# Self attention in a four-layer decoder: scores of four heads from split queries and keys in two float32r passes

## The chip, the cores and the metric

The kernel runs on one core of a Trainium2 chip, as one program. TensorE (PE in the rows, PEld for its weight loads) multiplies, VectorE (DVE) and ScalarE (ACT) read its results from eight PSUM banks, GpSimd (POOL) does small work, and SyncE (SP) issues transfers. The metric is the device time of one execution in microseconds; lower is better.

## The reference, cut to what matters

The reference is a decoder of four layers, each a cross attention and an FFN with experts. Only one piece is touched: the self attention that opens the second layer's FFN block. For each of 16 batches of 112 tokens with 256 channels (16 heads of 16):

```
h = layernorm(x, ln1_g, ln1_b)
qkv = (h @ Wqkv).reshape(Bb, Tt, H, 3 * hd)
q, k = (rope(q), rope(k))      # concat([t1*cos - t2*sin, t1*sin + t2*cos])
scores = jnp.einsum('bqhd,bkhd->bhqk', q, k) / math.sqrt(hd)
scores = jnp.where(causal, scores, -1e9)
probs = jax.nn.softmax(scores, axis=-1)
attn = jnp.einsum('bhqk,bkhd->bqhd', probs, v).reshape(Bb, Tt, d) @ Wproj
x = x + attn
```

## The kernel before

The stage `self_attention` lies at 950 to 1194 us of the profiled execution. It handles the 16 batches one after another; the heads of a batch go in four groups (g) of four. Each engine has an order written out by hand: `first` fills the pipeline, `heads(b, ...)` is run once a batch, and within it work on four batches is interleaved: scores, softmax and values of batch b, scores of groups 0 and 1 of b+1, normalisation and projection of b+2, first statistics of b+3, output of b-1. Counters (semaphores) join the engines; each engine takes its instructions strictly in its written order.

What happens to a batch, with the lines that count here:

- `project_qk` (PE, L2754) writes queries and keys of all heads to one bank; DVE's `rotate` (L2988 to L2992) applies the rotary embedding into `turned_q`.
- `turn_rotated` (PE, L2773) transposes `turned_q` in four pieces of 128 channels, two of queries and two of keys, so that channels lie on the rows. `take_queries` (ACT, L2897) copies the queries' half to `qT`.
- `spread_keys` (DVE, L3001) builds `keys`: for each of 16 heads a copy of the eight-head block of keys, multiplied by `headmask`, which is 0.25 on the head's own 16 rows and 0 on the others. With that a plain product over all 128 rows gives one head's scores, and the moving side carries four heads side by side (448 columns).
- `scores(b, g)` (PE) adds the causal mask by a bfloat16 product with the identity (L2786) and then the float32 product of `qT` and `keys` (L2788); the trace shows that one as two instructions.
- `group_max` (DVE, L3009) takes the maximum per head, `exps` (ACT, L2911) the exponential, `turn` and `take_probsT` (PE L2795, ACT L2918) transpose the probabilities, `values` (PE, L2807) multiplies with the values. `divide` (L3016, L3018), `turn_outputs`, `take_outputs`, `output` and `add` (L3027, L3029) finish the batch; `norm_1` to `norm_3` (L1038 to L1042, L2966), `turn_tokens` (PE, L2745) and `take_tokens` (ACT, L2886) prepare the next ones.

Two places in the written order matter. On DVE, `heads(b)` has `group_max(b, 2)`, `spread_keys(b+1)`, `group_max(b, 3)` in a row, and later `group_max(b+1, 0)`, `rotate(b+2)`, `group_max(b+1, 1)`, `norm_2(b+3)`, `add(b-1)`, `divide(b)`, `norm_3(b+3)`. On ACT the order is `exps(b, 2)`, `take_queries(b+1)`, `take_probsT(b, 1)`, `take_outputs(b-1)`, `exps(b, 3)`, `take_tokens(b+2)`; `project_qk(b+2)` waits for the last of these.

Of the kernel before, what the change touches and what calls it, by code (L numbers as in the profile page):

```python
# [6 lines left out]
F32 = mybir.dt.float32  # L7
# [3 lines left out]
F32R = mybir.dt.float32r  # L11
# [7 lines left out]
P = 128  # L19
# [2652 lines left out]
def self_attention(nc, core, name):  # L2672
# [8 lines left out]
    with ctx:  # L2681
# [8 lines left out]
        qT = [sb(f"qT{i}", [P, DC, T]) for i in range(2)]  # L2690
        keys = [sb(f"keys{i}", [P, H, T]) for i in range(2)]
# [18 lines left out]
        keys_ready, q_ready = core.counter("taken_K"), core.counter("taken_Q")  # L2710
        made = {c: core.counter(f"made_{c}") for c in "LVOY"}
# [11 lines left out]
        with nc.Block() as block:  # L2723
# [10 lines left out]
            def _(pe):  # L2734
# [13 lines left out]
                def project_qk(b):  # L2748
# [3 lines left out]
                    pe.wait_ge(rope_done.sem, rope_done.at(b.n))  # L2752
                    for k in range(DC):
                        ins = pe.matmul(psQK[0:T, 0:2 * D], hT[:, k, :], wqkv[:, k, 0:2 * D],  # L2754
                                        start=(k == 0), stop=(k == DC - 1))
# [10 lines left out]
                def turn_rotated(b, before_):  # L2766
# [5 lines left out]
                    for c in range(2 * DC):  # L2772
                        ins = pe.transpose(psR[:, c * T:(c + 1) * T],  # L2773
                                           turned_q[:, c * 8:(c + 1) * 8, :].rearrange("t h e -> t (h e)"),
                                           core.ident[0:T, 0:T])
                    ins.then_inc(r_made.sem, 1)

                def scores(b, g):
                    if g == 0:

                        pe.wait_ge(q_ready.sem, q_ready.at(b.n + 1))
                        pe.wait_ge(keys_ready.sem, keys_ready.at(b.n + 1))
# [5 lines left out]
                    pe.matmul(psS[g % 2][0:T, 0:G * T], qT[b.par][:, g // 2, :], keys[b.par][:, G * g:G * g + G, :],  # L2788
# [88 lines left out]
            def _(act):  # L2877
# [17 lines left out]
                def take_queries(b):  # L2895
                    act.wait_ge(r_made.sem, r_made.at(b.n + 1))
                    act.activation(qT[b.par][:, :, :], psR[:, 0:DC * T].rearrange("p (c t) -> p c t", t=T), ACT.Copy)\  # L2897
                        .then_inc(q_ready.sem, 1)
# [56 lines left out]
            def _(dve):  # L2955
# [24 lines left out]
                def rotate(b):  # L2980
# [4 lines left out]
                    def all_heads(t, lo, hi):  # L2985
# [6 lines left out]
                    dve.tensor_tensor(turned_q[:, :, :], turned_q[:, :, :], turned_by[:, :, :], ALU.add)\  # L2992
                        .then_inc(rope_done.sem, 1)

                def spread_keys(b):

                    dve.wait_ge(r_made.sem, r_made.at(b.n + 1))

                    dve.wait_ge(q_ready.sem, q_ready.at(b.n + 1))
                    for c in range(DC):  # L3000
                        ins = dve.tensor_tensor(keys[b.par][:, 8 * c:8 * c + 8, :],  # L3001
# [340 lines left out]
```

## Time and profile before

| | us |
|---|---|
| median of 3 runs | 3431.1 (3428.69 to 3436.66) |
| the profiled execution | 3437.43 |
| its span, first to last instruction | 3435.6 |
| self attention within it | about 950 to 1194 |
| PE, DVE, ACT busy over the whole span | 3106.0, 1658.8, 1563.6 |
| mean granted TensorE clock (1 is full) | 0.948 |

The stage is 7% of the time, and nothing outside of it changes but the numbers in a small table. So the whole-program shares say little about it; what has to be read is one period of the stage, from one `project_qk` to the next, engine by engine.

### The profile page before, as it was taken

What the parts mean: (1) busy time and instruction counts of PE and PEld (TensorE: products, weight loads), DVE (VectorE), ACT (ScalarE), POOL (GpSimd) and SP (SyncE); (2) the same over time, 40 slices, a digit from 0 to 9 for tenths busy, and PEclk for the clock granted to TensorE, in tenths of its full rate; (3) what the DMA queues carried; (4) which work ended last, traced back from release to release, by engine and by line L of the source; (5) the groups of instructions that cost most, each with busy time, mean ns of one, the idle gap of its engine ahead of it and who ended that gap; (6) DMA issues with size and microseconds to landing.
All of it is one profiled execution on the core that took longest, in us unless ns stands there. A gap on an engine that the chain in (4) does not pass through costs nothing. (4 is left out here: it accounts for less than half of the span.)

```text
span 3435.6 us, 60328 instructions
## 1 busy us (share of the span) xinstructions
PE 3106.0 (90%) x21966; PEld 2609.6 (76%) x21966; DVE 1658.8 (48%) x3470; ACT 1563.6 (46%) x4177; POOL 1319.2 (38%) x1417
## 2 busy tenths in 40 slices
PE   5888858998989869899999999598999999997999
PEld 4776748996756559778888887488788888876998
DVE  4777760003566557544444444301444444445766
ACT  2554523443345435445555555244555555552232
POOL 0000001112100022167777777211577777773433
PEclk8999969999999869999999999699999999996999
DMA  5555535552100044200000000464000000001332
GB/s 143 135 132 128 131 134 198 183 183 74 50 1 1 4 165 141 66 20 15 12 14 14 15 13 1 168 217 138 13 13 12 12 13 13 12 1 53 114 106 89
DMA packets 146134, 253.21 MB, mean 74 GB/s; under 512 B 46892, under 2 KB 122664, under 8 KB 133304
## 3 DMA queue, kind: packets, MB, share of 16 engines
q1 hardware_dynamic: 132216, 223.67, 21.7%
q0 software_dynamic: 8064, 20.20, 2.1%
q10 hardware_dynamic: 5568, 5.51, 0.5%
q8 instruction: 183, 3.00, 0.4%
q14 instruction: 103, 0.84, 0.1%
HBM read 214.85 MB, written 34.46 MB: 73 GB/s over the span
## 5 line engine op out<-in xcount | busy, mean ns | idle before, releaser
L719 POOL TENSOR_SCALAR L_probs<-L_probs,L_inverse 112x375 f32<-112x375 f32 x512 | 653.0, 1275 | 119.3 <-issue 119.3
L867 DVE TENSOR_REDUCE L_negmax<-bank 112x1 f32<-112x375 f32 x768 | 394.7, 542 | 428.1 <-PE bank L471 356.3
L675 ACT ACTIVATE L_probs<-bank,L_negmax 112x375 f32<-112x375 f32 x768 | 435.2, 572 | 216.7 <-DVE L_negmax L867 211.9
L498 PE MATMUL bank<-ident,L_probs 112*125 112x112 f32 x2304 | 399.4, 282 | 19.2 <-POOL L_probs L719 12.9
L498 PEld LDWEIGHTS bank<-ident,L_probs 112*125 112x125 f32 x2304 | 338.0, 189 | 91.1 <-issue 49.6
L717 POOL TENSOR_TENSOR L_inverse<-L_sums,neg_one 112x1 f32<-112x1 f32 x512 | 297.2, 580 | 141.4 <-ACT L_probs L675 141.1
L655 ACT ACTIVATE L_probsT<-bank 125x336 f32<-125x336 f32 x512 | 231.9, 453 | 248.4 <-PE bank L498 248.3
L637 ACT ACTIVATE v<-bank 125x512 f32<-125x512 f32 x192 | 114.8, 598 | 266.6 <-PE bank L424 266.6
L705 POOL TENSOR_TENSOR L_stats<-L_stats,neg_half 112x1 f32<-112x1 f32 x48 | 27.0, 563 | 520.6 <-DVE L_stats L784 520.6
L513 PE MATMUL bank<-L_probsT,v 125*64 125x112 f32 x3072 | 206.7, 270 | 1.8 <-ACT L_probsT L655 1.1
L417 PE MATMUL bank<-L_ctx_hi,L_wk_hi 128*128 128x376 f32 x512 | 149.5, 373 | 30.2 <-DVE L_ctx_lo L851 22.7
L513 PEld LDWEIGHTS bank<-L_probsT,v 125*64 125x64 f32 x3072 | 152.0, 138 | 31.0 <-issue 1.7
L1613 ACT ACTIVATE L0t_hidden<-bank,L0t_b 128x128 f32<-128x128 f32 x280 | 102.3, 368 | 143.6 <-PE bank L1578 126.0
L675 ACT ACTIVATION_READ_ACCUMULATOR L_probs<-bank,L_negmax 112x1 f32 x768 | 152.8, 199 | 0.0
L1578 PEld LDWEIGHTS bank<-L0t_xT,L0t_w 128*128 128x128 f32 x1120 | 133.3, 195 | 10.5 <-issue 8.8
L1578 PE MATMUL bank<-L0t_xT,L0t_w 128*128 128x128 f32 x1120 | 133.8, 279 | 8.0 <-issue 8.0
L809 DVE SCALAR_TENSOR_TENSOR L_keys_lo<-bank,L_bk,L_keys_hi 128x376 fp32r<-128x376 f32 x128 | 76.4, 607 | 131.8 <-ACT L_keys_hi L627 131.8
L1629 DVE TENSOR_TENSOR L0t_ys<-bank,L0t_b 128x256 f32<-128x256 f32 x35 | 14.9, 425 | 258.3 <-PE bank L1590 258.3
L424 PE MATMUL bank<-L_wv_hi,L_ctx_hi 128*125 128x512 f32 x384 | 137.8, 440 | 0.0
L809 DVE SCALAR_TENSOR_TENSOR L_keys_lo<-bank,L_keys_hi 128x376 fp32r<-128x376 f32 x128 | 68.8, 547 | 132.4 <-ACT L_keys_hi L627 131.9
L417 PE MATMUL bank<-L_ctx_hi,L_wk_lo 128*128 128x376 f32 x512 | 131.8, 339 | 0.0
L417 PE MATMUL bank<-L_ctx_lo,L_wk_hi 128*128 128x376 f32 x512 | 131.3, 338 | 0.0
(327 smaller groups left out, 7109.2 us busy)
## 6 DMA issues: line engine op xcount, KB each, us to landing
L0t_w<-in_F_w SPq DMA_DIRECT2D x35, 1024.0 KB, 4.9
L_keys<-spread_k SPq DMA_DIRECT2D x64, 376.0 KB, 6.7
L2t_w<-in_F_w SPq DMA_DIRECT2D x21, 1024.0 KB, 4.9
L_ctxT<-in_ctxT SPq DMA_DIRECT2D x48, 375.0 KB, 3.1
w_all<-in_F_w SPq DMA_DIRECT2D x16, 1024.0 KB
cap_w<-in_F_w SPq DMA_DIRECT2D x16, 1024.0 KB, 5.2
L3d_row<-comb_rows SPq DMA_DIRECT2D x64, 224.0 KB, 3.2
L_q<-spread_q SPq DMA_DIRECT2D x128, 56.0 KB, 2.2
```

The costliest lines, as they stand in the source:

```text
L417: ins = pe.matmul(bank[:, 0:SP], wt[:, k, m * P:(m + 1) * P], c[b.par][:, k, :], start=(n + k == 0), stop=(n + k == DC + 1))
L424: ins = pe.matmul(bank[0:SJ, 0:VW], c[b.par][:, k, j * SJ:(j + 1) * SJ], wt[:, k, vn * VW:(vn + 1) * VW], start=(n + k == 0), stop=(n + k ...
L498: ins = pe.transpose(psT[h % len(psT)][0:SJ, j * T:(j + 1) * T], probs[h % NB][:, j * SJ:(j + 1) * SJ], core.ident[0:T, 0:T])
L513: ins = pe.matmul(bank[i * dh:(i + 1) * dh, at:at + T], v[b.par][0:SJ, j, (h + i) * dh:(h + i + 1) * dh], probsT[(h + i) % NT][:, j, :], s ...
L637: ins = act.activation(v[b.par][0:SJ, j, n * VW:(n + 1) * VW], bank[0:SJ, 0:VW], ACT.Copy)
L655: act.activation(probsT[h % NT][:, :, :], psT[h % len(psT)][0:SJ, 0:J * T].rearrange("p (j t) -> p j t", t=T), ACT.Copy)\
L675: act.activation(probs[e % NB][:, :], psS[e % 2][0:T, 0:S], ACT.Exp, bias=negmax[b.par][:, e:e + 1], accum_out=sums[b.par][:, e:e + 1]).th ...
L717: pool.tensor_tensor(inverse[b.par][:, h:h + 1], sums[b.par][:, h:h + 1], core.neg_one[0:T, :], ALU.pow)
L719: pool.tensor_scalar(probs[h % NB][:, :], probs[h % NB][:, :], inverse[b.par][:, h:h + 1], None, ALU.mult)\
L809: dve.scalar_tensor_tensor(out=keys_lo[b.par][:, m, :], in0=bank[:, 0:SP], scalar=bk[:, m:m + 1] if biased else 0.0, in1=keys_hi[b.par][:, ...
L867: dve.tensor_reduce(negmax[b.par][:, h:h + 1], psS[h % 2][0:T, 0:S], AX, ALU.max, negate=True).then_inc(maxed.sem, 1)
L1578: ins = pe.matmul(psH[f % 4][:, 0:tile], w1[t % 2][:, k, f * P:(f + 1) * P], xT[:, k, :], start=(k == 0), stop=(k == DC - 1))
```

## The change

The float32 product of the scores becomes two products of float32r operands. The queries are split into a rounded part `q_hi` and the rest `q_lo`. A group's four heads are 64 channels; the rounded keys go to rows 0 to 63 and the rest of the keys to rows 64 to 127 of one operand. `q_hi` holds the same 64 channels on both halves of the rows, so that one pass gives q_hi times both parts of the keys, and a second pass over 64 rows adds q_lo times the rounded keys. For this the last instruction of `rotate` writes each group's channels twice (`twice`, 1024 elements a row in place of 512), `turn_rotated` has eight transposes in place of four (queries into the bank of `project_qk`, keys into the old one), ACT makes two rounded copies of 448 columns where it made one copy of 224, and DVE subtracts twice (64 rows) and multiplies by `headmask` in four pieces of 448 from SBUF in place of two of 896 from PSUM. The number of elements of `keys` is the same. `scores` waits for the keys group by group, and `project_qk` of the next batch also waits for `q_lo`, since the bank is shared.

```diff
@@ project_qk
                     pe.wait_ge(rope_done.sem, rope_done.at(b.n))
+                    pe.wait_ge(q_ready.sem, q_ready.at(b.n))
@@ turn_rotated
-                    for c in range(2 * DC):
-                        ins = pe.transpose(psR[:, c * T:(c + 1) * T],
-                                           turned_q[:, c * 8:(c + 1) * 8, :].rearrange("t h e -> t (h e)"),
-                                           core.ident[0:T, 0:T])
-                    ins.then_inc(r_made.sem, 1)
+                    for at, bank in ((0, psQK), (HG, psR)):
+                        for g in range(HG):
+                            ins = pe.transpose(bank[:, g * T:(g + 1) * T],
+                                               twice[:, at + g, :, :].rearrange("t i e -> t (i e)"), core.ident[0:T, 0:T])
+                        ins.then_inc(r_made.sem, 1)
@@ scores
                         pe.wait_ge(q_ready.sem, q_ready.at(b.n + 1))
-                        pe.wait_ge(keys_ready.sem, keys_ready.at(b.n + 1))
+                    pe.wait_ge(keys_ready.sem, keys_ready.at(HG * b.n + g + 1))
...
-                    pe.matmul(psS[g % 2][0:T, 0:G * T], qT[b.par][:, g // 2, :], keys[b.par][:, G * g:G * g + G, :],
+                    pe.matmul(psS[g % 2][0:T, 0:G * T], q_hi[b.par][:, g, :], keys[b.par][:, G * g:G * g + G, :],
+                              start=False, stop=False)
+                    pe.matmul(psS[g % 2][0:T, 0:G * T], q_lo[b.par][:, g, :], keys[b.par][0:64, G * g:G * g + G, :],
                               start=False, stop=True).then_inc(scored.sem, 1)
@@ take_queries
-                    act.wait_ge(r_made.sem, r_made.at(b.n + 1))
-                    act.activation(qT[b.par][:, :, :], psR[:, 0:DC * T].rearrange("p (c t) -> p c t", t=T), ACT.Copy)\
-                        .then_inc(q_ready.sem, 1)
+                    act.wait_ge(r_made.sem, r_made.at(2 * b.n + 1))
+                    act.activation(q_hi[b.par][:, :, :], psQK[:, 0:HG * T].rearrange("p (g t) -> p g t", t=T), ACT.Copy)\
+                        .then_inc(q_high.sem, 1)
+                    act.wait_ge(r_made.sem, r_made.at(2 * b.n + 2))
+                    act.wait_ge(keys_ready.sem, keys_ready.at(HG * b.n))
+                    act.activation(k_pair[:, :, :], psR[:, 0:HG * T].rearrange("p (g t) -> p g t", t=T), ACT.Copy)\
+                        .then_inc(k_high.sem, 1)
@@ rotate
-                    dve.tensor_tensor(turned_q[:, :, :], turned_q[:, :, :], turned_by[:, :, :], ALU.add)\
-                        .then_inc(rope_done.sem, 1)
+                    straight, crossed = (t[:, :, :].rearrange("t (g h) e -> t g (h e)", h=G).unsqueeze(2)
+                                         .broadcast_to([T, 2 * HG, 2, 64]) for t in (turned_q, turned_by))
+                    dve.tensor_tensor(twice[:, :, :, :], straight, crossed, ALU.add).then_inc(rope_done.sem, 1)
@@ spread_keys
-                    dve.wait_ge(r_made.sem, r_made.at(b.n + 1))
-                    dve.wait_ge(q_ready.sem, q_ready.at(b.n + 1))
-                    for c in range(DC):
-                        ins = dve.tensor_tensor(keys[b.par][:, 8 * c:8 * c + 8, :],
-                                                psR[:, (DC + c) * T:(DC + c + 1) * T].unsqueeze(1).broadcast_to([P, 8, T]),
-                                                headmask[:, :].unsqueeze(2).broadcast_to([P, 8, T]), ALU.mult)
-                    ins.then_inc(keys_ready.sem, 1)
+                    dve.wait_ge(q_high.sem, q_high.at(b.n + 1))
+                    dve.tensor_tensor(q_lo[b.par][:, :, :], psQK[0:64, 0:HG * T].rearrange("p (g t) -> p g t", t=T),
+                                      q_hi[b.par][0:64, :, :].bitcast(F32), ALU.subtract).then_inc(q_ready.sem, 1)
+                    dve.wait_ge(k_high.sem, k_high.at(b.n + 1))
+                    low = k_pair[64:P, :, :]
+                    dve.tensor_tensor(low, psR[64:P, 0:HG * T].rearrange("p (g t) -> p g t", t=T), low.bitcast(F32),
+                                      ALU.subtract)
+                    dve.drain()
+                    for g in range(HG):
+                        dve.tensor_tensor(keys[b.par][:, G * g:G * g + G, :],
+                                          k_pair[:, g, :].bitcast(F32).unsqueeze(1).broadcast_to([P, G, T]),
+                                          headmask[:, 0:G].unsqueeze(2).broadcast_to([P, G, T]), ALU.mult)\
+                            .then_inc(keys_ready.sem, 1)
```

On DVE, in the part of `heads` from the maximum of group 2 to that of group 1 of the next batch, the program of before has these rows (negmax rows are `group_max`, the `turned` rows `rotate`, the `stats` rows `norm_1`):

```order
L3009 TENSOR_REDUCE L1s_negmax0<-bank4 112x4
L3001 TENSOR_TENSOR L1s_keys1<-bank3,self_headmask_12 128x896 x2
L3009 TENSOR_REDUCE L1s_negmax0<-bank5 112x4
L1038 BN_STATS L1s_stats<-x 112x6
L1040 BN_AGGR L1s_stats<-L1s_stats 112x2
L1042 TENSOR_SCALAR L1s_stats<-L1s_stats 112x1
L3009 TENSOR_REDUCE L1s_negmax1<-bank4 112x4
L2988 TENSOR_TENSOR L1s_turned_by<-bank1,self_sin_10 112x32x8
L2989 TENSOR_TENSOR L1s_turned_by<-bank1,self_sin_10 112x32x8
L2990 TENSOR_TENSOR L1s_turned_q<-bank1,self_cos_9 112x512
L2992 TENSOR_TENSOR L1s_turned_q<-L1s_turned_q,L1s_turned_by 112x512
L3009 TENSOR_REDUCE L1s_negmax1<-bank5 112x4
```

The changed program has, in the same place:

```order
L3029 TENSOR_REDUCE L1s_negmax0<-bank4 112x4
L3012 TENSOR_TENSOR L1s_q_lo1<-bank1,L1s_q_hi1 64x448
L3017 TENSOR_TENSOR L1s_k_pair<-bank3,L1s_k_pair 64x448
L3021 TENSOR_TENSOR L1s_keys1<-L1s_k_pair,self_headmask_12 128x448 x4
L3029 TENSOR_REDUCE L1s_negmax0<-bank5 112x4
L1038 BN_STATS L1s_stats<-x 112x6
L1040 BN_AGGR L1s_stats<-L1s_stats 112x2
L1042 TENSOR_SCALAR L1s_stats<-L1s_stats 112x1
L3029 TENSOR_REDUCE L1s_negmax1<-bank4 112x4
L3001 TENSOR_TENSOR L1s_turned_by<-bank1,self_sin_10 112x32x8
L3002 TENSOR_TENSOR L1s_turned_by<-bank1,self_sin_10 112x32x8
L3003 TENSOR_TENSOR L1s_turned_q<-bank1,self_cos_9 112x512
```

Nothing has changed its place; two instructions between the maxima of groups 2 and 3 have become six. The row that follows these is the doubled last step of `rotate`, `L1s_twice`, 112x1024.

On ACT, from the exponentials of group 2 to the copy of the normalised tokens, before:

```order
L2911 ACTIVATE L1s_probs0<-bank4,L1s_negmax0 112x112 x4
L2897 ACTIVATE L1s_qT1<-bank3 128x224
L2918 ACTIVATE L1s_probsT1<-bank6 112x448
L2903 ACTIVATE L1s_oT<-bank0 128x224
L2911 ACTIVATE L1s_probs1<-bank5,L1s_negmax0 112x112 x4
L2886 ACTIVATE L1s_hT<-bank0,self_b_8,self_g_7 128x112 x2
```

and in the changed program:

```order
L2924 ACTIVATE L1s_probs0<-bank4,L1s_negmax0 112x112 x4
L2905 ACTIVATE L1s_q_hi1<-bank1 128x448
L2910 ACTIVATE L1s_k_pair<-bank3 128x448
L2931 ACTIVATE L1s_probsT1<-bank6 112x448
L2916 ACTIVATE L1s_oT<-bank0 128x224
L2924 ACTIVATE L1s_probs1<-bank5,L1s_negmax0 112x112 x4
L2894 ACTIVATE L1s_hT<-bank0,self_b_8,self_g_7 128x112 x2
```

One copy of 224 columns has become two of 448 ahead of the copy of the transposed probabilities.

## Rows read from the trace of the kernel before

**Rows 1.** Windows: one period; busy us (instructions) of each engine, then PE clock, DMA
```profile
1041.90:1056.19 14.29, 13.11 (x80) 9.34 (x80) 9.78 (x23) 7.88 (x26) 1.08 (x2) 1.00 0.00 1
```

**Rows 2.** Timeline, PE, one period: start us, duration us, engine, line, operation
```profile
1044.53 1.97 PE L2754 MATMUL bank<-self_wqkv,L1s_hT 128*112 128x512 f32 x4
...
1054.30 0.92 PE L2788 MATMUL bank<-L1s_keys,L1s_qT 128*112 128x448 f32 x2
1055.05 0.55 PE L2795 MATMUL bank<-ident,L1s_probs 112*112 112x112 f32 x4
1056.52 0.38 PE L2745 MATMUL bank<-ident,L1s_normed 112*128 112x112 f32 x2 [0.93 <-issue]
...
1058.82 0.68 PE L2754 MATMUL bank<-self_wqkv,L1s_hT 128*112 128x512 f32 x1
```

**Rows 3.** Timeline, DVE, the same period
```profile
1046.54 0.42 DVE L2988 TENSOR_TENSOR L1s_turned_by<-bank,self_sin 112x256 f32<-112x256 f32 x1 [1.57 <-PE bank L2754]
...
1047.21 0.68 DVE L2990 TENSOR_TENSOR L1s_turned_q<-bank,self_cos 112x512 f32<-112x512 f32 x1
1047.97 0.69 DVE L2992 TENSOR_TENSOR L1s_turned_q<-L1s_turned_q,L1s_turned_by 112x512 f32<-112x512 f32 x1
1048.58 0.62 DVE L3009 TENSOR_REDUCE L1s_negmax<-bank 112x4 f32<-112x448 f32 x1
...
1052.25 0.62 DVE L3009 TENSOR_REDUCE L1s_negmax<-bank 112x4 f32<-112x448 f32 x1
1054.35 2.09 DVE L3001 TENSOR_TENSOR L1s_keys<-bank,self_headmask 128x896 f32<-128x896 f32 x2 [1.48 <-ACT L1s_qT L2897]
1056.36 0.61 DVE L3009 TENSOR_REDUCE L1s_negmax<-bank 112x4 f32<-112x448 f32 x1
```

**Rows 4.** Timeline, ACT, the same period
```profile
1052.92 1.08 ACT L2911 ACTIVATE L1s_probs<-bank,L1s_negmax 112x112 f32<-112x112 f32 x4
1053.87 0.38 ACT L2897 ACTIVATE L1s_qT<-bank 128x224 f32<-128x224 f32 x1
1055.63 0.55 ACT L2918 ACTIVATE L1s_probsT<-bank 112x448 f32<-112x448 f32 x1 [1.38 <-PE bank L2795]
1056.07 0.35 ACT L2903 ACTIVATE L1s_oT<-bank 128x224 f32<-128x224 f32 x1
1057.01 1.09 ACT L2911 ACTIVATE L1s_probs<-bank,L1s_negmax 112x112 f32<-112x112 f32 x4 [0.58 <-DVE L1s_negmax L3009]
1057.97 0.80 ACT L2886 ACTIVATE L1s_hT<-bank,self_b,self_g 128x112 f32<-128x112 f32 x2
```

**Rows 5.** Lines L860 and L856: duration ns min/median/max, first and last start
```profile
L860 DVE TENSOR_TENSOR L_q_low<-L_q,L_q_high x64: 624/625/881, 1468.5 to 3069.9; 128x448 fp32r<-128x448 f32 x64
L856 DVE CAST L_q_high<-L_q x64: 393/394/727, 1468.0 to 3066.2; 128x448 fp32r<-128x448 f32 x64
```

**Rows 6.** Timeline, PE, expert stage: float32r passes of 448 columns
```profile
3251.52 0.37 PE L2275 MATMUL bank<-L3d_hid_hi,dense_w_hi 128*128 128x448 f32 x1
3251.73 0.37 PE L2275 MATMUL bank<-L3d_hid_lo,dense_w_hi 128*128 128x448 f32 x1
```

**Rows 7.** Timeline, PE: the first work after three idle stretches elsewhere
```profile
304.16 0.37 PE L484 MATMUL bank<-L_barred,ident_b 112*112 112x376 bf16 x1 [2.53 <-DMA L_q<-spread_q]
...
2426.66 0.61 PE L417 MATMUL bank<-L_ctx_hi,L_wk_hi 128*128 128x376 f32 x2 [1.88 <-DVE L_keys_lo L809]
...
1499.89 0.58 PE L498 MATMUL bank<-ident,L_probs 112*125 112x112 f32 x3 [1.74 <-POOL L_probs L719]
```

**Rows 8.** Windows around and behind these (columns as in rows 1)
```profile
304.10:307.60 3.50, 3.44 (x9) 2.25 (x10) 1.73 (x5) 0.67 (x2) 0.78 (x2) 0.56 0.12 45
...
2424.00:2428.00 4.00, 2.12 (x11) 1.45 (x9) 2.88 (x8) 2.15 (x6) 1.32 (x3) 0.95 0.00 0
2428.00:2432.00 4.00, 4.00 (x20) 3.45 (x20) 1.92 (x4) 2.40 (x7) 3.64 (x5) 0.62 0.02 4
...
1500.00:1504.00 4.00, 4.00 (x32) 2.94 (x33) 0.48 (x2) 1.05 (x2) 3.66 (x5) 1.00 0.00 0
```

More of the change, by code:

```diff
@@ L2689, in self_attention @@
         turned_by, turned_q = sb("turned_by", [T, 2 * H, 16]), sb("turned_q", [T, 2 * H, 16])
-        qT = [sb(f"qT{i}", [P, DC, T]) for i in range(2)]
-        keys = [sb(f"keys{i}", [P, H, T]) for i in range(2)]
+        q_hi = [sb(f"q_hi{i}", [P, HG, T], F32R) for i in range(2)]
+        q_lo = [sb(f"q_lo{i}", [P // 2, HG, T], F32R) for i in range(2)]
+        k_pair = sb("k_pair", [P, HG, T], F32R)
+        keys = [sb(f"keys{i}", [P, H, T], F32R) for i in range(2)]
+        twice = sb("twice", [T, 2 * HG, 2, 64])
         causal_b = sb("causal_b", [T, T], BF16)
@@ L2710, in self_attention @@
         keys_ready, q_ready = core.counter("taken_K"), core.counter("taken_Q")
+        q_high, k_high = core.counter("q_split"), core.counter("k_high")
         made = {c: core.counter(f"made_{c}") for c in "LVOY"}
@@ L3078, in self_attention @@
             s.stage_over(2 * B)
-        for s in (normed_ready, o_ready, qk_made, rope_done, r_made, keys_ready, q_ready, *made.values(), *taken.values()):
+        for s in (normed_ready, o_ready, qk_made, rope_done, q_high, k_high, q_ready, *made.values(), *taken.values()):
             s.stage_over(B)
+        r_made.stage_over(2 * B)
+        keys_ready.stage_over(HG * B)
         for s in (scored, maxed, exped, turned, probsT_ready, pv_done):
@@ L3265, in lay_out @@
     a["keys"] = np.arange(S, dtype=np.float32)
-    a["headmask"] = np.where(np.arange(P)[:, None] // 16 == np.arange(8)[None, :], 0.25, 0.0).astype(np.float32)
+    a["headmask"] = np.where(np.arange(P)[:, None] % 64 // 16 == np.arange(8)[None, :], 0.25, 0.0).astype(np.float32)
     for n in ("wq", "wk", "wv", "wo"):
```

## The prediction

> **What bounds the kernel now.** First the windows of one period of the stage: 14.29 us, of which TensorE is busy 13.11, 92%, and VectorE 9.78, 68% [rows 1]. Taken by busy time TensorE is the bound, and the change takes work from it. I did not stop there, because TensorE still stands idle 1.18 us in every period, always at the same places (0.93 us of it before `turn_tokens` [rows 2]); an engine that bounds a loop does not. The Trainium skill (Perfetto Trace Analysis, Identifying the Most-Contended Engine) says that matmul busy time is no good measure and to take the weight loads' share instead; here that is 9.34 us, 65%, which would put VectorE first. That is the same suspicion, but shares don't settle it either way.
>
> So next the timelines of the three engines over one period, followed link by link from `project_qk` to the next `project_qk`, each step from start to start:
>
> 1. `project_qk` starts on PE at 1044.53, `rotate` on DVE at 1046.54: 2.01.
> 2. `rotate`, 1046.54 to the start of `group_max(b+1, 1)` at 1048.58: 2.04.
> 3. From there DVE works without a gap up to the start of `group_max(b, 2)` at 1052.25, and the exponentials of that group start on ACT at 1052.92: 4.34. (It ends at 1052.87.)
> 4. The exponentials, 1052.92 to 1053.87, when the queries' copy starts behind them: 0.95.
> 5. The copy, to the start of `spread_keys` on DVE at 1054.35: 0.48.
> 6. `spread_keys`, to 1056.36: 2.01.
> 7. `group_max(b, 3)`, queued behind it on DVE; exponentials of group 3 at 1057.01; `take_tokens` at 1057.97; the next `project_qk` at 1058.82: 2.46.
>
> The sum is 14.29, the whole period [rows 2 to 4]. This loop closes through DVE and ACT; of PE it has only `project_qk`. The score passes, the transposes of probabilities and the value products aren't in it: they wait at `project_qk`, or at `turn_tokens`, for the loop. Both idle stretches of DVE (1.57 us waiting for `project_qk`, 1.48 us waiting for the queries' copy [rows 3]) are waits of the loop itself.
>
> **The change part by part.**
>
> *Scores (off the loop).* A float32 product of 448 columns takes 0.75 us (1054.30 to 1055.05 [rows 2]); a float32r pass of 448 columns takes 0.21 (3251.52 to 3251.73 [rows 6]). Two passes in place of it: 0.75 - 0.42 = 0.33 saved, four groups, 1.3 us a batch. The second pass has 64 rows; no row prices it apart, so I bound it by one wide pass and by the old 0.37 of half a float32 product. Either end changes nothing, since no score is on the loop.
>
> *Transposes (off the loop).* Four of the same kind (L2795) last 0.55, less what overlaps the next instruction [rows 2]. Four more cost 0.4 to 0.55 a batch; I take 0.4. PE's work goes from 13.1 to about 12.2 us a batch.
>
> *Last step of `rotate` (on the loop, link 2).* DVE's two-operand instruction takes 0.61 from start to start at 512 elements (1047.97 to 1048.58) and 2.01/2 = 1.005 at 896 [rows 3]: 1.03 ns an element. 512 more elements cost 0.53.
>
> *The queries' copy (link 5).* ACT copies 448 columns in 0.55, 224 in 0.38 [rows 4]: 0.17 more before DVE may start. The keys' copy follows at 0.44 (1055.63 to 1056.07); it ends 0.44 + 0.55 = 0.99 after the first one starts, and DVE needs it at 0.65 + 0.54 = 1.19. Hidden.
>
> *`spread_keys` (link 6).* At 448 elements an instruction takes 0.61 - 64 x 1.03 ns = 0.54 from start to start (the split's subtraction of another stage lasts 0.625 in all [rows 5], the same thing with the end that overlaps the next). Now: `q_lo` 0.54; `low` with the drain behind it 0.62 + 0.08 = 0.70 (the drain's 0.08 as between 1047.89 and 1047.97 [rows 3]); four products 4 x 0.54 = 2.16. In all 3.40 for 2.01: 1.39 more. That 64 rows in place of 128 save nothing I assume: every row works side by side, and there is no row with fewer; if it halved them it would be 0.5 less. The Trainium skill (VectorE: DVE Perf Modes, Two Vector instructions with no wait between them) has it that an instruction whose operands start in another quarter of the rows waits until all earlier ones are finished; `low` starts at row 64. No row here shows such a pair; by that rule the overlap of 0.08 is lost once more a batch, about 1 us in all.
>
> *New waits.* `project_qk(b+2)` waits for `q_lo(b+1)`, done 5 us earlier. `scores(b+1, 0)` waits for its own quarter of the keys; it comes behind `values(b, 1)`, late enough. The keys' copy waits for the last batch's keys, long done. The real queue is on DVE: `group_max(b, 3)` stands behind all six instructions, though its scores have been ready for a microsecond, and behind it wait `exps(b, 3)`, `take_tokens` and `project_qk`.
>
> *Sum of a lap.* 0.53 + 0.17 + 1.39 = 2.09; the period becomes 16.38 us. The loop is run for each `project_qk` in `heads`, 14 times: +29.3 us. Filling and draining the pipeline have one `spread_keys` more and cheaper scores; I take these as even, within 2 us.
>
> *The clock (added by the longer wait).* How long PE now idles before `project_qk`: counted from the start of the first copy, the probabilities' copy starts at 0.88 (two copies of 0.44); from its start to `turn_tokens` it was 0.89 (1055.63 to 1056.52) and from there to `project_qk` 2.30, now 1.97 with the cheaper score [rows 2, 4]. PE is free at 3.74. The loop arrives at 0.65 + 3.40 + 2.46 = 6.51. PE idles 2.8 us each lap, where it had nothing. What such gaps did in this trace: behind 2.53 and 1.88 us the granted clock fell to the lower level (1.2 of 2.4 GHz), 0.56 over the next 3.5 us in one case, 0.95 then 0.62 in the other; behind 1.74 us it stayed at 1.00 [rows 7, 8]. So I expect it to fall in most laps. The first case lost (1 - 0.56) x 3.5 = 1.5 us of PE's work at once; in the second, 0.05 x 4 = 0.2 us was lost before 2428, so it fell some 0.4 us before that, 0.9 after the restart. The first 1.8 us behind the gap are `project_qk`, which is on the loop: 1.5 us lost in the first manner, 0.9 in the second, nothing where the clock holds. What is slow behind it (`values`, a score) has over a microsecond to spare until `group_max(b+1, 1)`. I take 1.0 a lap, bounds 0 and 1.8: +14 us, bounds 0 and 25.
>
> *Total.* 29.3 + 14 = 43.3. Against the profiled execution, 3437.4, that is 3480.7. The median of the runs shown is 6.3 us lower, 3431.1, so for the median: 3474.4.
>
> **The rivals.**
>
> *A, the loop with a full clock:* +29.3, 3460.4. For it: the two low stretches came in other stages, and the work around the gap here is dense float32. Against: a gap of 1.88 was enough, and this one is 2.8.
>
> *B, the products into float32r run at the pace of a cast:* a cast of 448 elements lasts 0.394 where the subtraction lasts 0.625 [rows 5]. If the four products did so, 4 x 0.23 = 0.92 a lap is saved, the lap grows by 1.17, the total is +16.4 at full clock, 3447.5. Against it: the subtraction in that row also writes float32r, and is at the slow pace. The Trainium skill (VectorE: DVE Perf Modes, The perf-mode tier table) gives float32 two-operand instructions one element a cycle from SBUF as from PSUM, and the double pace only to those of one operand; by that B does not happen.
>
> *C, TensorE was the bound after all, and it gets faster:* then a lap falls by PE's saving, 1.3 - 0.4 = 0.9, 15 us over 16 batches, 3416. Place: PE's order between `project_qk` and the next. It decides only if the loop of DVE and ACT is shorter than PE's work, so from 13.1 us on down; I have it at 14.29 and growing. For it speaks the 92%; against it, that the seven links add up to the period without a rest.
>
> *D, no change:* some of the added DVE work would have to fall into DVE's own idle time (3.9 us a lap) without delaying `group_max(b, 3)`. The order rules it out: all of it stands before that instruction. Should a float32r pass cost 0.37, as half a float32 product, that still gives PE 13.5 us of work in a lap of 16.4: no change to my number.
>
> **How the numbers follow.** My forecast (loop and clock) 0.62; A 0.22; B 0.06; C 0.05; the rest 0.05, most of it between B and no change. The low end, 3455, holds A with a few microseconds less; the high end, 3488, is 29.3 + 25 with 2 or 3 us for the skill's rule and the ends of the stage. Outside are B, C and D and a longer tail above. 0.2% of the time is 7 us, about what can be told from no change here. Slower by more: forecast, A, B and most of the rest less some doubt, 0.91; no change 0.04; faster 0.05.
>
> **What the profile after would show.** Right: a period of some 17 us in the stage (16.4 where the clock holds); PE idle 2.5 to 3 us before `project_qk`, released by ACT's `hT`; `group_max(b, 3)` starting some 3.4 us after `q_lo`; the `twice` instruction at 1.2 us, the products at 0.6; float32r passes 0.21 apart; windows of 0.5 to 0.6 in PE's clock behind that gap. Wrong: a period under 14.3, PE idle time gone, or the gap before `project_qk` under a microsecond; then link 7 did not carry the delay. If the period grows but the clock stays at 1.00, only the last term was wrong.

## The result and the profile after

The changed kernel takes 3518.1 us (median of 4 runs, 3511.6 to 3524.7) and the kernel before 3431.1 (4 runs, 3428.7 to 3436.7): a ratio of 1.0258, 95% interval 1.0243 to 1.0272. It is slower, as predicted, but by 87 us and not by 43, and outside the predicted range (3455 to 3488). The profiled execution took 3515.3 with a span of 3513.5, 77.9 more than the profiled one before (which was 6 us above its median, where this one is 3 below); the granted clock over the whole span fell from 0.948 to 0.925.

The windows say where that is. The first row is one lap, from one `project_qk` to the next, and answers to [rows 1]; then come the steady laps, the filling and the draining of the pipeline.

```profile
1095.16:1115.20 20.04, 17.48 (x84) 11.72 (x84) 11.98 (x26) 8.27 (x27) 1.09 (x2) 0.76 0.00 1
1000.00:1230.00 230.00, 205.74 (x996) 138.40 (x995) 139.84 (x305) 98.56 (x306) 12.49 (x23) 0.76 0.00 1
950.00:1000.00 50.00, 42.02 (x155) 26.52 (x153) 28.89 (x60) 17.35 (x54) 2.71 (x5) 0.64 0.00 1
1230.00:1278.00 48.00, 41.04 (x192) 29.39 (x192) 18.54 (x37) 17.42 (x55) 0.00 (x0) 0.68 0.00 1
```

The same view of the kernel before, for its two ends (the second from its last `turn_tokens` to the next stage; between the ends the clock is 1.00):

```profile
950.00:1000.00 50.00, 41.89 (x217) 27.30 (x218) 33.19 (x72) 22.21 (x72) 3.80 (x7) 0.94 0.00 1
...
1157.22:1196.05 38.83, 32.83 (x188) 24.17 (x188) 14.66 (x29) 16.79 (x54) 0.00 (x0) 0.86 0.00 1
```

The lap was 14.29 and is now about 20 us, and the clock column has gone from 1.00 to 0.76. By the starts of `turn_tokens` the stage divides as follows. From its first one to the first of the steady laps it took 948.63 to 985.07 before and 946.75 to 996.66 after: 13.5 us more. Twelve laps took 172.1 (to 1157.22) and take 233.6 (to 1230.25): 61.4 more, 19.47 us a lap on average, in single laps 17.2 to 20.7. From there to the first instruction of the next stage, 38.8 and 48.0: 9.2 more. That is 84 us in this stage. It began 1.9 earlier, and the rest of the program gave back 4.

TensorE over one such lap:

```profile
1095.16 3.75 PE L2759 MATMUL bank<-self_wqkv,L1s_hT 128*112 128x512 f32 x4 [2.22 <-ACT L1s_hT L2894]
...
1105.62 0.35 PE L2792 MATMUL bank<-L1s_causal_b,ident_b 112*112 112x448 bf16 x1
1105.64 0.52 PE L2794 MATMUL bank<-L1s_keys,L1s_q_hi 128*112 128x448 f32 x1
1106.10 0.46 PE L2796 MATMUL bank<-L1s_keys,L1s_q_lo 64*112 64x448 f32 x1
1106.49 0.60 PE L2803 MATMUL bank<-ident,L1s_probs 112*112 112x112 f32 x4
...
1111.14 0.38 PE L2749 MATMUL bank<-ident,L1s_normed 112*128 112x112 f32 x2 [0.93 <-issue]
...
1115.20 2.05 PE L2759 MATMUL bank<-self_wqkv,L1s_hT 128*112 128x512 f32 x2 [1.63 <-ACT L1s_hT L2894]
```

The new wait before `project_qk` is there, released by ACT's `hT`. Behind it `project_qk` takes 3.75 us instead of the 1.97 of [rows 2]. The granted clock around it in short windows:

```profile
1092.80:1093.60 0.80, 0.14 (x2) 0.00 (x0) 0.80 (x2) 0.25 (x1) 0.00 (x0) 0.97 0.00 0
1093.60:1094.40 0.80, 0.00 (x0) 0.00 (x0) 0.65 (x4) 0.80 (x5) 0.18 (x1) 0.50 0.00 0
...
1103.40:1104.00 0.60, 0.60 (x5) 0.44 (x3) 0.31 (x2) 0.60 (x4) 0.00 (x0) 0.68 0.00 0
1104.00:1113.00 9.00, 8.07 (x59) 6.05 (x57) 6.17 (x14) 3.76 (x11) 0.55 (x1) 1.00 0.00 1
```

It falls to the lower level, 1.2 GHz, already inside the gap, and comes back at about 1103.8: ten microseconds low, half the lap, with TensorE busy all the time from 1095.16 on. A mean of 0.76 over the steady laps says the same of all of them: 48% of the time at half clock, 9.3 us of each 19.47. (Not all laps look alike: in some, as at about 1032.1, 1073.1 and 1151.6, the clock falls already around `turn_tokens`, and the gap before `project_qk` is then at most 0.5 us.) What this does on DVE and ACT:

```profile
1098.95 0.42 DVE L3001 TENSOR_TENSOR L1s_turned_by<-bank,self_sin 112x256 f32<-112x256 f32 x1 [4.29 <-PE bank L2759]
...
1101.74 0.62 DVE L3029 TENSOR_REDUCE L1s_negmax<-bank 112x4 f32<-112x448 f32 x1
...
1106.60 0.62 DVE L3029 TENSOR_REDUCE L1s_negmax<-bank 112x4 f32<-112x448 f32 x1 [0.50 <-PE bank L2796]
1109.12 0.62 DVE L3012 TENSOR_TENSOR L1s_q_lo<-bank,L1s_q_hi 64x448 fp32r<-64x448 f32 x1 [1.90 <-ACT L1s_q_hi L2905]
...
1112.73 0.62 DVE L3029 TENSOR_REDUCE L1s_negmax<-bank 112x4 f32<-112x448 f32 x1
```

```profile
1102.67 0.54 ACT L2931 ACTIVATE L1s_probsT<-bank 112x448 f32<-112x448 f32 x1 [6.14 <-PE bank L2803]
...
1107.57 1.08 ACT L2924 ACTIVATE L1s_probs<-bank,L1s_negmax 112x112 f32<-112x112 f32 x4
1108.52 0.57 ACT L2905 ACTIVATE L1s_q_hi<-bank 128x448 fp32r<-128x448 f32 x1
```

The seven links of this lap are 3.79, 2.79, 5.83, 0.95, 0.60, 3.61 and 2.47; the sum is 20.04. Links 4, 5 and 7 are as forecast (0.95, 0.65, 2.46), link 6 is 0.2 longer than its 3.40. Link 1 is `project_qk` at half clock. Link 2 is 0.22 over its 2.57. Link 3, which I had as DVE alone (4.34), now waits for TensorE: `exps(b, 1)` stands on ACT behind the copy of transposes that TensorE made late, and `group_max(b, 2)` itself waits 0.50 for a score pass.

### The profile page after: what moved, and what is told of

Same layout as the page of the kernel before. It is cut to its first block and busy times, and to the rows that moved or that the text cites. A ratio compares the mean times of both kernels' runs of the same rounds, so it can differ in the third digit from the quotient of the medians.

```text
span 3513.5 us, 60600 instructions
## 1 busy us (share of the span) xinstructions
PE 3172.1 (90%) x22030; PEld 2650.8 (75%) x22030; DVE 1703.5 (48%) x3534; ACT 1570.3 (45%) x4193; POOL 1315.9 (37%) x1417
## 6 DMA issues: line engine op xcount, KB each, us to landing
w_all<-in_F_w SPq DMA_DIRECT2D x16, 1024.0 KB, 13.5
```

## The experiments

The question is where the 3 us a lap beyond the forecast loop come from: the loop is longer than its links said, or the clock costs three times what I took. Then, what lets the clock fall. The four sessions ran the kernel before again, at 3429.7 (runs 1 to 4), 3434.3 (5 to 8), 3431.5 (9 to 11) and 3429.7 (12); each ratio is against its own session. Line numbers differ by a few between kernels.

**1. The gap before `project_qk` filled** with twelve bf16 products into its own bank.

```diff
 def project_qk(b):
-    pe.wait_ge(taken["L"].sem, taken["L"].at(b.n + 1))
     pe.wait_ge(rope_done ...)
     pe.wait_ge(q_ready ...)
+    for _ in range(12):
+        pe.matmul(psQK[0:T, 0:G * T], ident_b, causal_b x 4, start=True, stop=True)
+    pe.wait_ge(taken["L"].sem, taken["L"].at(b.n + 1))
```

> The changed kernel with 12 extra bfloat16 products of 448 columns (0.19 us each, 2.2 us) into the bank of project_qk, issued while TensorE would idle before project_qk; their results are overwritten. Theory 'clock': the gap lets the granted clock fall, the low stretch lasts about 10 us of every 20 us lap and carries everything beyond the lengthened loop; filled, the clock stays at 1.00, the lap is the 16.4 us of the links and the time is before + 29, about 3460. Rival 'other waits' (the extra 2.7 us a lap are waits of DVE and ACT that only look like clock): the time stays at about 3518, or grows with the extra work.

Measured: 3511.6, ratio 1.0238 (1.0219 to 1.0256), some 7 us less than the changed kernel and hardly to be told from it (the two intervals overlap). The theory missed by 50 us, and the rival's number is near without its reason. The gap is closed, and the clock falls all the same:

```profile
1070.97 0.38 PE L2749 MATMUL bank<-ident,L1s_normed 112*128 112x112 f32 x2 [0.93 <-issue]
...
1073.59 3.72 PE L2757 MATMUL bank<-L1s_causal_b,ident_b 112*112 112x448 bf16 x12
```

```profile
1072.00:1073.00 1.00, 1.00 (x5) 0.48 (x5) 1.00 (x3) 0.00 (x0) 0.00 (x0) 0.89 0.06 16
1073.00:1076.00 3.00, 3.00 (x11) 2.06 (x11) 1.94 (x6) 2.19 (x8) 0.54 (x1) 0.50 0.00 0
1076.00:1078.00 2.00, 2.00 (x9) 1.11 (x8) 0.00 (x0) 0.99 (x5) 0.00 (x0) 0.95 0.00 0
```

It goes at about 1072.8, 1.8 us after the end of the 0.93 us before `turn_tokens` that had been there all along. In this lap it is low for some 3.4 us, in the next (from about 1089.9) for 6.8; laps alternate between 18.0 and 19.6. So one filled gap is not enough, and my picture of one gap with one stretch behind it is wrong.

**2. In the changed kernel, `group_max(b, 3)` ahead of `spread_keys(b + 1)`.** This takes the added DVE work out of the way of the last maximum.

```diff
 group_max(b, 2)
+group_max(b, 3)
 if after:
     spread_keys(b + 1)
-group_max(b, 3)
```

> The changed kernel with group_max(b, 3) ahead of spread_keys(b+1) on DVE, nothing else. Theory 'loop': project_qk hangs on group_max(b, 3), which no longer waits behind the six instructions; its links shrink by 0.54 + 0.70 + 2.16 = 3.4 us, TensorE's own work and its wait at turn_tokens set the lap, about 13.5 to 14, so the time is 5 to 10 us under before: 3421 to 3426, if the clock holds. If the gap at turn_tokens (some 1.5 us) is enough to drop the clock, up to 40 more. Rival 'DVE is simply too full' (its total work bounds the lap, whatever the order): stays within 10 us of 3518.

Measured: 3472.7, ratio 1.0132 (1.0107 to 1.0158): 45 us back, which rules out the rival, and still 7 us above what the theory allowed with a clock that falls. Idle time before `project_qk` is gone, and some laps are 14.4 us (1064.54 to 1078.95); others are up to 17.6, where the clock falls. One such place:

```profile
1076.36 0.38 PE L2749 MATMUL bank<-ident,L1s_normed 112*128 112x112 f32 x2 [0.93 <-issue]
...
1078.95 3.49 PE L2759 MATMUL bank<-self_wqkv,L1s_hT 128*112 128x512 f32 x4
```

Its only idle stretches are 0.93 and 0.10 us, hardly more than the kernel before has, where the clock held.

**3. The same step in the kernel before.**

> The kernel before with group_max(b, 3) ahead of spread_keys(b+1). Theory 'loop': the old order had the keys ready just as TensorE wanted them (scores of b+1 start 1.1 us after the keys end), so delaying the keys behind the maximum, which must wait for its scores until 1055.3, moves them 1.5 us later and TensorE waits about 0.4 us a lap: 3437, slightly slower. Rival 'this order is better anyway': faster by the 0.05 us a lap or more that project_qk waits, 3420 to 3430.

Measured: 3452.3, ratio 1.0065 (1.0046 to 1.0083), 15 us above the theory's 3437: the 0.4 us a lap came as expected, the fall of the clock was not expected. From `turn_tokens` to `turn_tokens` a lap is 14.70 where the clock holds (1042.76 to 1057.45 is one) and 16.38 where it falls (1057.45 to 1073.83), five and seven of twelve; the clock over 1000 to 1150 is 0.93. It falls behind a second short wait of 0.35 us that stands beside the 0.93.

**4. The kernel before, its two key products issued twice** with a drain between: 2.16 us more on the loop and nothing else.

```diff
-for c in range(DC):
+for c in 2 * list(range(DC)):          # a drain ahead of the second round
     ins = dve.tensor_tensor(keys[...], psR[...], headmask[...], ALU.mult)
```

> The kernel before with the two products that build the keys issued twice (the same values, a drain between): DVE's part of the loop grows by 2.1 us a lap, as much as the change adds, while TensorE's work stays that of before (float32 scores). Theory 'loop': +2.1 x 14 = +29 at a full clock, 3460; and TensorE then idles about 2.1 us before project_qk, over the 1.9 us behind which the clock was seen to fall, so with the clock as in the changed kernel up to +90, 3520. Rival 'it is the float32r passes or the new copies': then this kernel stays within 10 us of before.

Measured: 3477.6, ratio 1.0142 (1.0122 to 1.0161), 48 us more. On DVE the products and the drain take 4.17 us from their start to `group_max(b, 3)` (995.38 to 999.55), where they took 2.01:

```profile
995.38 4.25 DVE L3004 TENSOR_TENSOR L1s_keys<-bank,self_headmask 128x896 f32<-128x896 f32 x4 [1.49 <-ACT L1s_qT L2897]
```

Three laps of the profile are 16.45 or 16.46 (985.56 to 1002.01 is one), which is 14.29 + 2.16: the loop passes added DVE work on in full. Other laps are 17 to 21, and the clock over 1000 to 1150 is 0.90. So the same delay without any part of the change does more than half of its damage (48 of 87 us).

**5. The changed kernel with both gaps filled:** the twelve products, and five ahead of `turn_tokens`.

```diff
 if after2:
+    pe.wait_ge(exped.sem, exped.at(HG * b.n + 3))
+    for _ in range(5):
+        pe.matmul(psS[0][0:T, 0:G * T], ident_b, causal_b x 4, start=True, stop=True)
     turn_tokens(b + 2, prior)
```

> The changed kernel with the 12 extra products before project_qk and 5 more (0.9 us) in the idle time before turn_tokens, into a score bank that is free then; all of them are overwritten. Theory 'thin stretch' (formed on the run with one gap filled, in which the clock fell at the scores behind turn_tokens, ahead of the filled gap: the changed kernel does too little TensorE work around turn_tokens, where the float32 score of before did more): with both filled the clock stays at 1.00, the lap is the 16.4 us of the links, time before + 29, 3460. Rival 'the fillers only add work': 3510 or more, as with one gap filled.

Measured: 3486.0, ratio 1.0147 (1.0121 to 1.0173). The first row is a lap, the second the steady stretch, the others the two ends:

```profile
1065.39:1081.95 16.56, 16.56 (x103) 11.45 (x102) 11.70 (x26) 8.50 (x27) 1.08 (x2) 1.00 0.00 1
...
1000.00:1193.00 193.00, 192.72 (x1180) 133.48 (x1179) 136.05 (x303) 98.34 (x301) 12.43 (x23) 1.00 0.00 1
...
950.00:1000.00 50.00, 44.75 (x213) 29.60 (x212) 29.33 (x61) 19.05 (x59) 2.97 (x6) 0.85 0.00 1
1193.00:1240.00 47.00, 42.16 (x204) 30.44 (x203) 18.41 (x36) 17.58 (x56) 0.00 (x0) 0.69 0.00 1
```

The time lies between the theory's 3460 and the rival's 3510: the laps are nearly as the theory had them, the ends of the stage are not. With the clock at 1.00 the lap is 16.56 by measurement and 16.38 by the prediction's links. This run separates the two terms: of the 5.2 us that a lap grew, 2.27 are the loop and 2.9 the clock. (TensorE has no idle time left in this lap, but link 7 is 2.48 where it was 2.47 in the changed kernel, so the products do not hold `project_qk` up.) The links of this lap are read from its DVE and ACT rows:

```profile
1067.40 0.42 DVE L3007 TENSOR_TENSOR L1s_turned_by<-bank,self_sin 112x256 f32<-112x256 f32 x1 [2.50 <-PE bank L2761]
...
1069.97 0.62 DVE L3035 TENSOR_REDUCE L1s_negmax<-bank 112x4 f32<-112x448 f32 x1
...
1075.86 0.62 DVE L3018 TENSOR_TENSOR L1s_q_lo<-bank,L1s_q_hi 64x448 fp32r<-64x448 f32 x1 [1.59 <-ACT L1s_q_hi L2911]
1076.51 0.63 DVE L3023 TENSOR_TENSOR L1s_k_pair<-bank,L1s_k_pair 64x448 fp32r<-64x448 f32 x1
1077.21 2.23 DVE L3027 TENSOR_TENSOR L1s_keys<-L1s_k_pair,self_headmask 128x448 fp32r<-128x448 f32 x4
1079.47 0.62 DVE L3035 TENSOR_REDUCE L1s_negmax<-bank 112x4 f32<-112x448 f32 x1
```

```profile
1074.30 1.09 ACT L2930 ACTIVATE L1s_probs<-bank,L1s_negmax 112x112 f32<-112x112 f32 x4 [0.47 <-DVE L1s_negmax L3035]
1075.27 0.56 ACT L2911 ACTIVATE L1s_q_hi<-bank 128x448 fp32r<-128x448 f32 x1
```

**6. Run 2 with the five products ahead of `turn_tokens`.**

> The changed kernel with group_max(b, 3) ahead of spread_keys(b+1), and the 5 extra products before turn_tokens. Theory 'thin stretch': the clock stays at 1.00 nearly throughout, the lap is 13.5 to 14.3 and the time 3420 to 3431, where the same order without the fillers took 3473. Rival 'DVE and ACT bound this order': 3460 to 3475, the fillers change nothing.

Measured: 3448.9, ratio 1.0040 (1.0024 to 1.0057). The clock is 1.00 over 1000 to 1150 and every lap 14.33. Of the 43 us that run 2 still lost, products that compute nothing give back two thirds. The rest, which the theory did not have, is at the ends of the stage: in the profiles the twelve steady laps take 172.0 us (172.1 in the kernel before), the filling 6.5 more and the draining 9.0 more.

**7. Run 6 with `group_max(b, 2)` also moved ahead of `norm_3(b + 2)`.**

> As the run before, with group_max(b, 2) also ahead of norm_3(b+2). Theory 'loop': 0.3 us a lap less before the exponentials of group 2, 3416 to 3427; the best version that the links point to. Rival: norm_3 later makes TensorE wait at turn_tokens instead, no gain over the run before.

Measured: 3449.3, ratio 1.0041 (1.0027 to 1.0054). No gain over run 6, and laps of 14.33 again: with the maxima out of the way of `spread_keys` the DVE order is not what sets the lap. What does set the 14.33, no run tests.

**8. The kernel before with cheaper scores alone:** `qT` and `keys` held as float32r, each float32 product replaced by two float32r passes of the same operands. The remaining parts of the operands are left out, and DVE and ACT do what they did.

```diff
-pe.matmul(psS[g % 2][...], qT[...], keys[...], start=False, stop=True).then_inc(scored.sem, 1)
+for last in (False, True):
+    ins = pe.matmul(psS[g % 2][...], qT[...], keys[...], start=False, stop=last)
+ins.then_inc(scored.sem, 1)
```

> The kernel before with queries and keys held as float32r and the score product as two float32r passes of the same operands: the remaining parts are left out and the product is added twice, so the scores are another thing. DVE's and ACT's instructions, their number and size stay those of before; only TensorE's work falls, by 0.33 us a group. Theory 'thin stretch': with nothing added anywhere, the cheaper scores alone let the clock fall in many laps, and the time rises by 10 to 50 us. Rival 'only the long gap before project_qk does it': the clock stays at 1.00 and the time within 5 us of before.

Measured: 3444.0, ratio 1.0026 (1.0008 to 1.0044). Cheaper scores make the kernel slower, by some 9 us (0.1 to 0.4%), just under the theory's 10 to 50. Where the clock holds, the laps are 14.28 or 14.29 (985.29 to 999.58 to 1013.86), no shorter than before; what TensorE saves turns into idle time before `project_qk`, and behind it the clock falls in some laps, which are then 15.7:

```profile
999.58 1.97 PE L2754 MATMUL bank<-self_wqkv,L1s_hT 128*112 128x512 f32 x4 [1.12 <-ACT L1s_hT L2888]
...
1005.65 0.35 PE L2786 MATMUL bank<-L1s_causal_b,ident_b 112*112 112x448 bf16 x1
1005.68 0.73 PE L2789 MATMUL bank<-L1s_keys,L1s_qT 128*112 128x448 f32 x2
1006.25 0.55 PE L2797 MATMUL bank<-ident,L1s_probs 112*112 112x112 f32 x4
```

The laps are only part of the loss. The first row is the steady stretch; the second goes from the last `turn_tokens` to the next stage, and the third is the same stretch of run 12, where the freed time is filled:

```profile
1000.00:1150.00 150.00, 129.17 (x803) 99.55 (x802) 97.10 (x220) 79.87 (x254) 10.82 (x20) 0.93 0.00 1
...
1160.21:1205.81 45.60, 38.47 (x188) 30.89 (x188) 15.72 (x31) 16.69 (x54) 0.00 (x0) 0.66 0.00 1
...
1159.85:1195.28 35.43, 29.31 (x204) 23.38 (x204) 14.53 (x30) 16.75 (x54) 0.00 (x0) 0.98 0.00 1
```

Twelve laps take 5.4 us more than before, the drain 6.8 more: it is 45.6 us at a clock of 0.66, where the kernel before has 38.8 at 0.86 and run 12 has 35.4 at 0.98.

**9. The changed kernel with only the five products ahead of `turn_tokens`,** the counterpart of run 1.

> The changed kernel with five short bf16 products ahead of turn_tokens only; the 2.5 us before project_qk stay empty. What each gap does by itself. Theory (the clock falls wherever TensorE's work is thin for long enough; both places matter): the gap before project_qk alone still lets it fall in most laps, behind the gap, in project_qk: laps of 17 to 20 us, window 1000:1190 at 0.80 to 0.95, time 3500 to 3515. Rival (only the thin stretch around turn_tokens starts the fall): laps 16.5 and the clock at 1.00 without the twelve products, time 3480 to 3488, as with both gaps filled.

Measured: 3522.5, ratio 1.0277 (1.0262 to 1.0293), above theory and rival and not to be told from the changed kernel. From the fifth lap on all are 20.4 or 20.5, so that filling this gap alone even lengthens them (19.47 on average in the changed kernel). In 0.5 us windows the clock falls at 1046, after less than a microsecond of idling in the gap before `project_qk`:

```profile
1045.00:1045.50 0.50, 0.10 (x2) 0.00 (x0) 0.40 (x2) 0.50 (x3) 0.00 (x0) 1.00 0.00 0
1045.50:1046.00 0.50, 0.00 (x0) 0.00 (x0) 0.45 (x2) 0.50 (x4) 0.21 (x1) 0.97 0.00 0
1046.00:1046.50 0.50, 0.00 (x0) 0.00 (x0) 0.24 (x1) 0.50 (x3) 0.33 (x1) 0.50 0.00 0
```

With runs 1 and 5: either gap by itself lets the clock fall, and in the changed kernel both have to be closed.

**10. Run 8 with the five products ahead of `turn_tokens`.**

> The kernel before with each float32 score product replaced by two float32r passes of the same operands (the remaining parts are left out, nothing is added on DVE or ACT), and five bf16 products ahead of turn_tokens. Without the five it took 3444, 9 us more than before. Theory (those 9 us are the clock alone): it stays at 1.00 in 1000:1150, laps 13.6 to 14.3, time 3425 to 3436. Rival (the 9 us come from something else in the two passes, as a start later behind them): time unchanged, 3440 to 3447, with the clock at 1.00.

Measured: 3438.7, ratio 1.0019 (1.0008 to 1.0030), clock 0.97 over 1000 to 1150. It still falls in some laps (1055.60 to 1071.31 is one, 15.71 us), where the 1.1 us before `project_qk` is still open; the others are about 14.28. The time lies between the theory and the rival, and both had the clock at 1.00. It can't be told from run 8 either: the intervals overlap, and the drain, which these products don't reach, is 45.5 us as there.

**11. Control: the kernel before with the same five products.**

> Control: the kernel before with the same five bf16 products ahead of turn_tokens, each lap. Its clock is at 1.00 in the steady laps anyway. Theory: the products find idle time, laps stay 14.29, time within 4 us of before (3430 to 3438), a few us less if they hold the clock in the first and last laps. Rival (the products cost time by themselves, by delaying turn_tokens): 13 laps by 0.3 us or more, 3438 or above.

Measured: 3425.8, ratio 0.9992 (0.9981 to 1.0004): no difference that can be told, though some 4 us under the range expected. The products cost nothing by themselves, and where the clock holds anyway they bring nothing.

**12. Run 8 with the mask's product issued three times a group,** which fills what the cheaper scores opened. (Each has `start=True`, so only the last one counts.)

```diff
-pe.matmul(psS[g % 2][...], ident_b, causal_b x 4, start=True, stop=False)
+for last in (False, False, True):
+    pe.matmul(psS[g % 2][...], ident_b, causal_b x 4, start=True, stop=not last)
```

> The kernel before with each float32 score product as two float32r passes of the same operands (remaining parts left out), as in the run at 3444, and the bf16 product of the mask issued three times in each group instead of once. The two passes took 0.35 us less a group than the float32 product (0.60 from mask to transposes against 0.95), which opened 1.12 us of idle time before project_qk; two more mask products of about 0.21 us fill it again. Theory (what lets the clock fall is TensorE's idle time, not the kind of product): gap before project_qk under 0.1, clock at 1.00 in 1000:1150, laps 14.29, time 3427 to 3436. Rival (float32r passes by themselves let it fall, whatever stands beside them): clock 0.90 to 0.95 there as without the filling, time 3440 to 3447. Third (the mask product is on the way of the maxima): clock 1.00 but laps of 14.7 or more.

Measured: 3432.0, ratio 1.0007 (0.9995 to 1.0019), not to be told from before.

```profile
1000.00:1150.00 150.00, 137.23 (x914) 107.46 (x912) 101.21 (x228) 82.78 (x263) 11.35 (x21) 1.00 0.00 1
```

Clock 1.00, laps 14.34 (for 14.29), the idle time before `project_qk` gone. So float32r passes as such do not slow the clock; what they leave empty does.

## Why the prediction was right in sign and wrong in size

*What bounds the kernel.* Right. That the loop runs through DVE and ACT, with TensorE not in it but for `project_qk`, is shown from both sides: work added to DVE alone lengthens the lap by its full 2.16 us (run 4), and work taken from TensorE alone shortens it by nothing (run 8). Rival C is dead by run 8.

*The sum of a lap.* Right to 0.2 us. With the clock held the links are 2.01, 2.57, 4.33, 0.97, 0.59, 3.61 and 2.48 (run 5), and only link 6 is off by more than 0.1, 3.61 for 3.40. In it `q_lo` takes 0.65 from start to start where I had 0.54, `low` with its drain 0.70 as forecast, and the four products 2.26 where I had 2.16, which is the subtraction's pace and not the cast's: rival B did not happen. The 0.65 shows no overlap between `q_lo` and `low`, which start at different rows. By the rule of the Trainium skill that the prediction cited (VectorE: DVE Perf Modes, Two Vector instructions with no wait between them), it should be so; the trace agrees, at 0.1 us.

*The scores.* Off the loop, as I said, but my price was wrong. I had two passes of 0.21 each for 0.75, a saving of 0.33 a group. From the mask's product to the transposes the changed kernel takes 0.87 (1105.62 to 1106.49), run 8 takes 0.60 (1005.65 to 1006.25), and the kernel before 0.95 (1008.07 to 1009.02 in its timeline). The saving is 0.08. In the rows the weights of the pass of 64 rows are not loaded beside the running pass of 128:

```profile
1105.62 0.18 PEld L2794 LDWEIGHTS bank<-L1s_keys,L1s_q_hi 128*112 128x112 f32 x1
1106.10 0.17 PEld L2796 LDWEIGHTS bank<-L1s_keys,L1s_q_lo 64*112 64x112 f32 x1 [0.30 <-issue]
1106.49 0.38 PEld L2803 LDWEIGHTS bank<-ident,L1s_probs 112*112 112x112 f32 x4 [0.22 <-issue]
```

The load waits 0.30 us for no semaphore, and the next one, back at 112 rows, 0.22. In run 8, where both passes have 128 rows, the pair of loads starts at once and nothing waits behind it. The Trainium skill (TensorEngine Tiling (Array Packing), Key Properties) says that changing the tiling mode drains TensorE; these rows fit it, though whether a pass of 64 rows is such a change no run tested apart. It did not matter for the lap, as forecast; it made the gap before `project_qk` 2.4 us at full clock (the twelve products of run 5 take 2.43) and not the 2.8 I had worked out.

*The clock: the step that failed.* I took 1.0 us a lap, bounds 0 and 1.8. Measured, it is 2.9 a lap in the steady laps (19.47 less 16.56), 35 us over twelve of them. By the fourteen laps of the forecast (from the second `project_qk` to the last) the kernel before takes 203.3 us, run 5 235.9 and the changed kernel 277.6: the loop is 32.6 where I had 29.3, the clock 41.7 where I had 14. Three parts of the working were wrong. First, the length: I read from [rows 8] that a fall lasts 3.5 us and costs the first `project_qk`. Here it is low for 9.3 us a lap, 4.7 us of TensorE's work, of which 2.9 reach the lap. Second, what is exposed: I wrote that what is slow behind `project_qk` "has over a microsecond to spare until `group_max(b+1, 1)`". At half clock the work behind `project_qk` is late by more than that; link 3 grew by 1.5 and link 2 by 0.2, beside 1.8 in link 1. Third, the place: I thought of one gap. Of the three gaps in [rows 7] that I went by, the two of 1.88 and 1.74 us seemed to mark a bound that the old 0.93 us was far below. But in run 1 the clock fell 1.8 us behind exactly that 0.93, and in run 9 it fell before the other gap was a microsecond old. Three isolated gaps from other stages could not stand for gaps that return in every lap.

*"Either end changes nothing, since no score is on the loop."* This is the sentence whose logic failed. It holds for the loop and not for the clock: run 8 changes nothing but the scores and is 9 us slower, and run 12, which fills what they freed, is not.

*The ends of the stage: a second term that failed.* I took filling and draining as even within 2 us. By the starts of `turn_tokens` they cost 13.5 + 9.2 us more than before (clock 0.64 and 0.68, where it was 0.94 and 0.86); two of the fourteen laps of the forecast lie in that filling, and what lies outside of all fourteen is still 2.5 + 7.3, 9.8 us where I had none. Run 5, whose products don't reach the drain, still took 49.5 us from its last `turn_tokens` to the next stage, against 38.8 before. For the drain run 8 points to a cause: it adds nothing on DVE or ACT, only the scores are cheaper, and its drain is 6.8 us longer at a clock of 0.66; with the freed time filled (run 12) it is 3.4 shorter than before. So cheaper scores alone can cost most of what the drain lost; that they do in the changed kernel, whose passes save 0.08 us a group where those of run 8 save 0.35, is likely and not shown. How the loss in the filling divides into added DVE work and clock, no run separates.

*The total.* Twelve laps with the clock held would be 198.7 (12 x 16.56), 26.6 more than before; with the clock as it was they are 34.9 more still; the ends 22.7; the earlier start and the rest of the program give back 6.2. That is 78.0 by the profiled executions, where I had 29 + 14. Of the 35 us between the two the clock of the fourteen laps is 28, the ends 10, the loop 3, less the 6. Rival A, the loop with a full clock at 3460, is what run 5 nearly is, but that one lies at 3486 for its ends.

*What stays open.* In run 2 the clock falls with 0.93 and 0.10 us of idle time, and in the kernel before it never falls in the steady laps with 0.93. The rows call TensorE busy for 13.4 of 14.4 us (run 2, 1064.54 to 1078.95) and for 13.1 of 14.3. In run 3, which has no split passes, a third wait of 0.35 us was enough. A likely reason for run 2 is that busy rows of the split passes hide the 0.30 and 0.22 us in which weights are waited for; that is argued and not shown.

## What to carry to other kernels

Follow the loop link by link and sum it; that part could be trusted to 0.2 us in 16, and it told in advance that cheaper products would bring nothing. But work taken from an engine off the loop is not free to take when that engine is TensorE: ask of each change what it leaves empty there, and count every idle stretch of the lap together, the old ones too, since a gap that was harmless may not be so once another stands near it (run 3) or the work around it is another (run 1). Look at the filling and draining of a pipeline too: there the loop does not bound, and in run 8 the drain lost more than the laps. When a clock term enters a forecast, price the whole stretch at the lower level, with everything in it that then comes onto the loop, and give it a range as wide as that; and if a lap has to be long, filling TensorE with idle products can pay: five a lap cost nothing (run 11), and seventeen brought back 35 us in the twelve laps of run 5.

## What the runs showed of the hardware that was not expected

- The granted clock fell to 1.2 of 2.4 GHz 1.8 us behind an idle stretch of 0.93 us (run 1), and 0.9 us into an idle stretch (run 9), with TensorE busy over 85% of the lap; in the kernel before the same 0.93 us did not, in any window of its steady laps.
- Once low, it stayed so for about ten microseconds of full work in the changed kernel (1093.6 to 1103.8), and for about 3.4 in single laps of runs 1 and 2.
- A float32r pass of 64 rows behind one of 128 takes 0.39 us to the next instruction, and the one of 128 ahead of it 0.46, where two passes of 128 rows take 0.57 together (run 8).
- Cheaper score passes alone drained the pipeline 6.8 us later (run 8: 45.6 us at a clock of 0.66 for 38.8 at 0.86).
